# Experts' tiles: the row normalisation of the second next tile, ahead of the sums of the current tile

## The reference, cut to what matters

```
logits = t @ switch_w + switch_b;  route_prob_max, routes = max, argmax of softmax(logits)
for e in range(8):
    h = gelu(t @ w1[e] + b1[e])          # 256 -> 1024
    y = h @ w2[e] + b2[e]                # 1024 -> 256
    out = where(routes == e, y, out)
x = x + out * route_prob_max
```

## Time and profile before

| what | value |
|---|---|
| median of 3 runs | 2945.3 us (2940.83 to 2946.29) |
| the profiled execution's own time | 2946.05 us |
| its span in the trace | 2944.2 us |
| PE busy in the span | 2482.5 us (84%) |
| DVE busy | 2186.6 us (74%) |
| ACT busy | 1941.3 us (66%) |
| POOL busy | 1638.1 us (56%) |
| mean granted TensorE clock | 0.921 of full |

### The profile page before, as it was taken

The page is one execution under the profiler, slowest core; times in us unless marked ns, Lnnn a source line. Parts: engine busy times, 40 slices in busy tenths (PEclk is TensorE's granted clock), DMA queues, the critical chain, the costliest instruction groups (busy, mean ns, idle before and its releaser), DMA issues. The chain is left out here.

```text
span 2944.2 us, 97775 instructions
## 1 busy us (share of the span) xinstructions
PE 2482.5 (84%) x38790; PEld 1909.7 (65%) x38790; DVE 2186.6 (74%) x4938; ACT 1941.3 (66%) x4321; POOL 1638.1 (56%) x1710
## 2 busy tenths in 40 slices
PE   3999999999839999949699999999668887477776
PEld 2777777777626777735477777777556666354544
DVE  4999999999848999963567777777758885544444
ACT  2888888888739999914367777777646664334343
POOL 3777777677434555510077666666357775344443
PEclk9999999999959999979899999999879995588888
DMA  5222222222000000000032232222100003100000
GB/s 152 69 69 72 79 69 74 71 68 79 14 14 1 1 1 1 1 31 1 20 93 76 67 81 81 67 77 81 43 12 16 16 18 120 31 30 26 30 27 22
DMA packets 126748, 140.20 MB, mean 48 GB/s; under 512 B 17568, under 2 KB 115648, under 8 KB 125152
## 3 DMA queue, kind: packets, MB, share of 16 engines
q1 hardware_dynamic: 118448, 123.60, 14.4%
q0 software_dynamic: 3744, 10.31, 1.1%
q10 hardware_dynamic: 4112, 0.07, 0.1%
HBM read 123.78 MB, written 10.16 MB: 45 GB/s over the span
## 5 line engine op out<-in xcount | busy, mean ns | idle before, releaser
L2110 DVE TENSOR_TENSOR_SCAN m_s<-m_a,m_psBx 128x2048 f32<-128x2048 f32 x64 | 282.8, 4418 | 21.6 <-PE m_psBx L1885 18.8
L1397 DVE SCALAR_TENSOR_TENSOR ew_w<-x_psS,ew_w 128x1024 f16<-128x1024 f32 x128 | 156.3, 1221 | 136.6 <-ACT ew_w L1298 136.6
L676 ACT ACTIVATE x_prob<-x_prob,x_low 128x257 f32<-128x257 f32 x512 | 254.5, 513 | 4.7 <-DVE x_low L802 3.1
L1896 PE MATMUL m_psS<-m_s,all_ident 128*128 128x256 f32 x1024 | 238.1, 386 | 0.9 <-DVE m_s L2110 0.9
L3100 DVE SCALAR_TENSOR_TENSOR all_xres<-e1t_psH,e1t_bias,all_xres 128x128 f32<-128x128 f32 x312 | 87.9, 344 | 201.2 <-ACT all_xres L3020 201.2
L1896 PEld LDWEIGHTS m_psS<-m_s,all_ident 128*128 128x128 f32 x1024 | 190.5, 191 | 43.3 <-issue 18.2
L802 DVE CUSTOM_DVE_ANT_0 x_prob<-x_psS,x_masked,x_prob 128x256 f32<-128x256 f32 x512 | 216.2, 478 | 0.7 <-PE x_psS L558 0.5
L2017 ACT ACTIVATE m_a<-m_dt,m_rate 128x248 f32<-128x248 f32 x512 | 206.0, 491 | 5.0 <-DVE m_s L2110 4.6
L3058 POOL TENSOR_TENSOR e1t_hidl<-all_xres,e1t_hidh 128x512 f16<-128x512 f32 x78 | 96.3, 1234 | 198.6 <-ACT e1t_hidh L3032 195.9
L691 ACT ACTIVATE x_kh<-x_psK,x_bk 128x256 f16<-128x256 f32 x256 | 107.5, 470 | 131.0 <-PE x_psK L442 131.0
L1118 PE MATMUL x_psV<-x_wvh,ew_w 128*128 128x256 f16 x1024 | 189.9, 274 | 0.0
(11 more groups left out here) (539 smaller groups left out, 9328.0 us busy)
## 6 DMA issues: line engine op xcount, KB each, us to landing
x_ctx<-in_ctxT SPq DMA_DIRECT2D x64, 1024.0 KB, 7.1
x_mraw<-in_mask SPq DMA_DIRECT2D x128, 128.5 KB, 2.7
x_stage<-in_L_ffn_w SPq DMA_DIRECT2D x32, 256.0 KB, 3.7
e1r_stage<-in_L_ffn_w SPq DMA_DIRECT2D x8, 1024.0 KB, 4.9
all_xres<-in_x SPq DMA_DIRECT2D x1, 4096.0 KB, 14.5
ew_w<-x_vx SPq DMA_DIRECT2D x128, 32.0 KB, 5.7
e_x<-all_xres SPq DMA_DIRECT2D x32, 128.0 KB, 1.9
x_vxr<-x_vx SPq DMA_DIRECT2D x96, 8.0 KB, 2.3
```

The costliest lines, as they stand in the source:

```text
L676: act.activation(prob[c % 4][:, h, :], prob[c % 4][:, h, :], ACT.Exp, bias=low[c % 4][:, h:h + 1], scale=-1.0, accum_out=sm[c % 2][:, h:h ...
L1397: dve.scalar_tensor_tensor(pT[c % 4][1][:].rearrange("p r k n -> p (r k n)"), psS[c % 2][:], PS, pT[c % 4][0][:].rearrange("p r k n -> p ( ...
L1896: last = pe.matmul(psS[:, h * ST:(h + 1) * ST], con["ident"][:], S[h][:, :, m, :], start=m == 0, stop=m == NS - 1)
L2110: dve.tensor_tensor_scan(rows(S), rows(A), psBx[:], 0.0, ALU.mult, ALU.add).then_inc(scan_done, 1)
```

## The change

DVE's round calls `normalise(s + 2)` directly behind `lo_xn(s + 1)`, ahead of both `add_bias` calls of tile s, where it stood behind them. No instruction, wait, buffer or semaphore is added or taken away. The streams of the other engines are the same.

```diff
             for s in range(SLOTS + 2):
                 if s + 1 < SLOTS:
                     lo_xn(s + 1)
+                if s + 2 < SLOTS:
+                    normalise(s + 2)
                 if s < SLOTS:
                     add_bias(s, 0)
                     add_bias(s, 1)
-                if s + 2 < SLOTS:
-                    normalise(s + 2)
                 if s >= 2:
                     finish(s - 2)
```

## The result

| | before | changed |
|---|---|---|
| median | 2945.8 us (2940.83 to 2948.16, 4 runs) | 2815.2 us (2813.07 to 2819.07, 4 runs) |
| ratio | | 0.956, 95% interval 0.9544 to 0.9577 |
| span of the profiled execution | 2944.2 us | 2814.6 us |
| mean granted clock | 0.921 | 0.934 |

The account below looks back on a forecast made before the run. No engine was full: PE waited 75.3 us for DVE's normalise, and its clock fell after each pause. Rounds 119.7, last 1.5 and first two 5.0, 126 us in all, gave 2819 us; range 2798 to 2850.

Parts of the forecast that it names:

- The inputs: DVE's normalise at its new place: lo_xn ends at +4.03, rows land with 0.9 to 1.9 us left.
- What it delays: First half's sums on DVE: normalise ends at +4.44, sums start at +4.50, so it lies wholly in DVE's idle time.
- the cover behind them: Slack between the first half's sums on DVE and PE's need of them: the first 1.9 us of delay cost nothing.
- The sums at +4.8: DVE's normalise meets POOL's lo_hid at a shared port, slips to +4.40, sums to +4.8; the 1.9 us absorb it.
- PE's round: PE from transposes to transposes: 6.5 us, first product 0.90 after the transposes; 5.95 at best.
- The clock: PE's clock in the experts' rounds: stays high without the 2 us pause; low clock costs 1.56 us in 32 rounds, 50.
- the cross-check of 75 and 50: Gain by cause in the experts' tiles: PE's pause 75.3 us and the low clock 50, together 125.
- The sum: Gain over the experts' rounds: 35 rounds 119.7 us, last round 1.5, first two 5.0; in all 126.
- B: Rival on PE's clock: the pause goes, the low clock stays, only 75.3 us gained: 2871 us; chance 0.07.
- E: Rival: nothing changes, PE's transposes wait for something else that ends as late as normalise: 2945 us; chance 0.03.
- C: Rival: another engine, POOL or DVE's queue, becomes the bound and stretches the round to 7.5 us: 2855 us; chance 0.08.
- D: Rival: slower; normalise at the head of DVE's queue waits for its gather, a ring over two rounds: 2974 us; chance 0.02.

Follow-up runs that it names:

- e5: Changed kernel with gathers two tiles ahead in place of three (EARLY = 2): 2929.3 us.
- e6: Kernel before the change with gathers two tiles ahead in place of three (EARLY = 2): 2944.3 us.
- e7: Changed kernel with PE's load of the next expert's number behind the fourth k of the round in place of behind the transposes: 2812.1 us.
- e3: Kernel before the change with eight added matmuls, read by nothing, ahead of the transposes of each round from the third on: 2894.9 us.
- e8: Changed kernel with one small added gelu ahead of ACT's first work, so that its table is loaded early: 2811.4 us.
- e4: Kernel before the change with the normalisation behind the first of the second half's four sums, shortening PE's pause: 2896.6 us.
- e1: Kernel before the change with the normalisation between the sums of the two halves: 2813.6 us.
- e2: Kernel before the change, DVE's order kept, with PE's transposes and expert's number load moved behind the third k of the round: 2812.0 us.
- e10: Kernel before the change with four added matmuls ahead of the transposes of each round from the third on, in place of e3's eight: 2899.1 us.

## Why the prediction was right, by its steps

*The inputs.* As forecast: `lo_xn`, then the normalisation, with no wait for a gather behind the first two. e5 and e6 show the cover of the gathers from the other side.

*What it delays.* Forecast +4.44 for its end and +4.50 for the sums. With t = 0 at ACT's low copy of the round before, it ends at +4.47 and the sums start at +4.39, overlapping its end, and PE doesn't notice:

```profile
2698.91 0.60 ACT L3020 ACTIVATE all_xres<-e1t_psH 128x512 f32<-128x512 f32 x1 [2.34 <-PE e1t_psH L2978]
...
2702.40 0.59 ACT L3020 ACTIVATE all_xres<-e1t_psH 128x512 f32<-128x512 f32 x1
```

The times are right, but the forecast that it lies wholly in DVE's idle time is not quite: the low copy that the sums need starts at 2702.40, by the forecast's 0.69 they could have started at 2703.09, and they start at 2703.30, directly behind the normalisation. The 0.2 us are hidden by the cover behind them. DVE's idle time ahead of the sums, forecast at about 60 us, is 57.5, in its two parts:

```profile
  ACT all_xres L3020: 34.9, 28
  issue: 22.6, 15
```

The normalisation took 0.51 us where it had taken 0.40: it did meet POOL (last section). The sums at +4.8 that the prediction drew from that meeting didn't come.

*PE's round.* Forecast 6.5, measured 6.31. The first product came 0.7 us behind the transposes in the mean of the rounds in place of 0.90; my reading is that part of the load of the expert's number now passes while PE still works. The lower bound that I gave, 5.95, would have needed the whole load hidden, and e7 shows that the stream doesn't run that far ahead.

*The clock.* The two causes were priced at 75 and 50 us. e3 measures the second by itself: 49. The rest of the 130.6 us is 82. The 75 was too high for the pause: 6.4 of it is the wait for the first tile's rows, which stayed, and 67.2 went (75.3 to 8.1). So some 14 us are shorter joints, which the cross-check of 75 and 50 did not have: the transposes now start 0.16 us before the last second product ends (2705.00 + 0.27 against 2705.11), and the first product follows them sooner. That the cross-check came to 125 is in part luck; the sum itself goes by whole rounds and holds without it.

*The sum.* 35 rounds between the third and the last transposes: 347.29 before, 222.60 after (2558.82 to 2781.42), so 124.7 for the 119.7 forecast, of which 6.6 is the shorter round and -1.7 the one slow round behind the table load. The first two rounds gave 4.0 for 5.0: I had not seen the table load in their midst; the second round took 6.06 us with it and 4.97 in e8 without. The last gave 1.5, as forecast.

*The rivals.* B is refuted by the clock of 1.00, E by the 130 us. e4 shows that B was not far off: a noted pause of 1.07 us a round was enough for the clock to fall in 18 of 35, so that the clock would hold with only the gaps of issue left was an inference from another layer that came true, not one that rows of this stretch had shown. C didn't come: POOL was busy 4.6 us in a round of 6.4. D is real as a mechanism, with its price as worked out for e5 (9.5 against 9.6 us), but needs its gathers one tile later.

## What to carry to other kernels

Where two in-order streams meet once in a round, look for what the awaited instruction stands behind: here 0.4 us of work with long-landed inputs waited behind sums that needed the waiting engine's own last product, and either stream could have been reordered. Price a pause of PE twice, by its length and by the time at half clock behind it, and take the second from rounds of the same trace in which the clock happened to hold. Before adding up waits that a change is to remove, take out those that it can't (here the first, 6.4 us). Before moving a step forward, count how long its input has been there: the same edit with its gathers one tile later would have given 14 us instead of 130.

## What the runs showed of the hardware that was not expected

VectorE and GpSimd met. The prediction said that no row showed the shared port pair of the Trainium skill's page "SBUF — State Buffer", section "SBUF: two separate sides". The changed kernel's rows fit it. `lo_hid` of POOL and the last instruction of `finish` on DVE, which reads two tiles from SBUF:

```profile
2700.77 2.46 POOL L3058 TENSOR_TENSOR e1t_hidl<-all_xres,e1t_hidh 128x512 f16<-128x512 f32 x2 [1.66 <-ACT e1t_hidh L3032]
...
2701.50 0.71 DVE L3113 SCALAR_TENSOR_TENSOR all_xres<-e1t_yb,e1t_row 128x256 f32<-128x256 f32 x1
```

It takes 0.71 us and ends 0.28 behind the first of the pair's two halves (2700.77 + 1.16); before it took 0.49 in the median, and POOL's instruction 1.24 each where it now takes 1.16. In e5 it starts 0.27 us earlier in POOL's instruction, takes 0.98 and ends the same 0.28 behind it: its end hangs on POOL's, not on its own start. The normalisation went from 0.405 to 0.515 where it meets the second half, ending 0.15 behind it, and stayed at 0.405 in e1, where it meets none, and in e2, where it starts ahead of POOL. That fits the page's rule that whoever comes second waits for the end of the other's instruction; it wasn't tried by itself.

The clock depends on more than the length of the pause: e4 and e10 differ by 0.1 us in it, by 0.90 to 0.98 in the clock, and by 0.8 us in the length of the rounds at the high clock, and e10 has four matmuls more ahead of each pause. Which of these does it, or how the pauses fall in time, stays open. The Trainium skill's page "TensorE: Matmul & The Clock Gate", section "A second HAM failure mode: psum-queue depth-cycling", which tells of short idles that make the clock swing, fits e4 and not the changed kernel.
